# Grouped-query attention between two adapter layers: keys turned by blocks on VectorE, softmax sums divided out of the output, rotary table loaded per unit, four weight stage slots

## The reference

```
x += down(silu(gate(x)) * up(x))            # layer 0, F = 1376, each with a rank-16 adapter chosen per sequence
q, k, v = x Wq', x Wk', x Wv'               # layer 1: 32 query heads, 8 key heads, D = 128
q, k = rope(rmsnorm(q)), rope(rmsnorm(k))   # positions: length of the sequence + token
keys = [paged cache: 16 pages of 32, through a table; k]      # 640 keys, those past the length masked
x += softmax(q keys' / sqrt(D)) [cached v; v] Wo'
x += x (W2 quantised by group, codebook, + adapter)'          # layer 2, 512 x 512
x += x W3[adapter]'                                           # layer 3, one of 8 matrices
```

## Time and profile before

| | |
|---|---|
| median of 3 runs | 1479.15 us (1478.11 to 1483.87) |
| the profiled execution | 1478.15 us, its span 1476.5 us |
| mean granted TensorE clock | 0.985 |
| layer 0 up to the first projection of q | 276.7 us |
| 64 units, to the last step's end | some 1137 us |
| layers 2 and 3 | some 62 us |

### The profile page before, as it was taken

The page is one execution under the profiler, slowest core; times in us unless marked ns, Lnnn a source line. Parts: engine busy times, 40 slices in busy tenths (PEclk is TensorE's granted clock), DMA queues, the critical chain, the costliest instruction groups (busy, mean ns, idle before and its releaser), DMA issues.

```text
span 1476.5 us, 26919 instructions
## 1 busy us (share of the span) xinstructions
PE 1407.4 (95%) x8068; PEld 1218.9 (83%) x8068; DVE 1147.7 (78%) x2779; ACT 994.3 (67%) x1985; POOL 504.4 (34%) x688
## 2 busy tenths in 40 slices
PE   6998998789999999999999999999999999999888
PEld 5776776568888888888888888888888888888767
DVE  4885666467788788888888888788888878888756
ACT  5664663366677777767777776777777777777643
POOL 5321221245434333334433333343333434333200
PEclk9999999889999999999999999999999999999999
DMA  8776765324321111212111211121111212110224
GB/s 191 245 236 188 247 186 161 101 83 136 116 72 43 58 47 42 62 41 59 57 54 34 65 44 51 36 65 45 58 51 37 61 47 58 51 37 29 101 77 152
DMA packets 102852, 130.01 MB, mean 88 GB/s; under 512 B 11973, under 2 KB 78150, under 8 KB 97334
## 3 DMA queue, kind: packets, MB, share of 16 engines
q1 hardware_dynamic: 97184, 108.70, 23.7%
q0 software_dynamic: 5376, 19.60, 4.7%
q10 hardware_dynamic: 150, 0.01, 0.0%
HBM read 125.11 MB, written 36.72 MB: 110 GB/s over the span
## 4 chain that ended last, share of the span: by engine, by line
PE 78%; DVE 8%; ACT 5%; issue 4%; DMA 3%; POOL 1%; POOLq 1%; SPq 0%; ACTq 0%; DVEq 0%
PE proj_ps L1278 18%; PE sc L1318 15%; PE o_ps L1355 14%; PE proj_ps L1376 12%; PE ring L1337 9%; PE o_ps L1089 2%; PE ring L1391 2%; PE ring L1403 2%; PE proj_ps L1089 2%; PE sc L1089 2%; ACT wb L725 2%; DMA prep<-scale_dram 1%; DMA wd_raw<-in_WdT 1%; DVE pTl L1837 1%; DVE wb L1546 1%
## 5 line engine op out<-in xcount | busy, mean ns | idle before, releaser
L1837 DVE TENSOR_TENSOR pTl<-ring,pTh 128x512 fp32r<-128x512 f32 x320 | 215.1, 689 | 79.1 <-ACT pTh L914 74.1
L896 ACT ACTIVATE p_sb<-p_sb,bias,rstd 128x640 f32<-128x640 f32 x256 | 235.8, 921 | 43.8 <-DVE bias L1813 43.8
L649 POOL TENSOR_TENSOR rstd<-var,half_neg 128x4 f32<-128x4 f32 x64 | 86.0, 1344 | 493.7 <-DVE var L1874 493.7
L914 ACT ACTIVATE pTh<-ring 128x512 fp32r<-128x512 f32 x320 | 184.4, 599 | 53.1 <-PE ring L1337 52.3
L1803 DVE CUSTOM_DVE_ANT_0 p_sb<-sc,mask 128x640 f32<-128x640 f32 x256 | 209.2, 817 | 2.5 <-PE sc L1318 2.1
L1337 PE MATMUL ring<-ident,p_sb 128*128 128x128 f32 x1280 | 182.1, 273 | 5.5 <-DVE p_sb L1829 3.0
L1278 PE MATMUL proj_ps<-wh,xh 128*128 128x512 f32 (+1 forms) x512 | 179.6, 351 | 0.7 <-ACT q_sb L941 0.7
L1337 PEld LDWEIGHTS ring<-ident,p_sb 128*128 128x128 f32 x1280 | 153.4, 141 | 32.6 <-DVE p_sb L1829 3.7
L1278 PE MATMUL proj_ps<-wl,xh 128*128 128x512 f32 (+1 forms) x512 | 173.1, 338 | 0.0
L1278 PE MATMUL proj_ps<-wh,xl 128*128 128x512 f32 (+1 forms) x512 | 172.6, 337 | 0.0
L1318 PE MATMUL sc<-kTh,qTh 128*128 128x320 f32 x512 | 164.4, 321 | 2.5 <-DVE kTl L1938 2.5
(11 more groups left out here) (242 smaller groups left out, 3696.4 us busy)
## 6 DMA issues: line engine op xcount, KB each, us to landing
k_pages<-in_k_cache SPq DMA_DIRECT2D x128, 128.0 KB, 3.1
v_pages<-in_v_cache POOLq DMA_DIRECT2D x128, 128.0 KB, 3.2
k_raw<-k_pages SPq DMA_DIRECT2D x64, 256.0 KB, 3.0
v_raw<-v_pages SPq DMA_DIRECT2D x64, 256.0 KB, 2.9
stage<-in_Wqkv SPq DMA_DIRECT2D x32, 384.0 KB, 3.5
w_raw<-in_WguT SPq DMA_DIRECT2D x19, 512.0 KB, 5.1
stage<-in_WoT SPq DMA_DIRECT2D x32, 256.0 KB, 3.4
w_raw<-in_W3T SPq DMA_DIRECT2D x8, 1024.0 KB, 5.0
```

Source lines behind the costliest of these rows:

```text
L896: act_e.activation(p_sb[:, p_slot(u, h), :], p_sb[:, p_slot(u, h), :], ACT.Exp, bias=bias[:, h:h + 1], scale=rstd[:, u.k % 2, h:h + 1], ac ...
L914: act_e.activation(pTh[:, c, :], ring[c % 2][:, :], ACT.Copy).then_inc(S["pth"], 1)
L1837: v.tensor_tensor(pTl[:, c, :], ring[c % 2][:, :], pTh[:, c, :].bitcast(F32), ALU.subtract).then_inc(S["ptl"], 1)
```

## The change

- Cached keys are no longer transposed by PE. `load_k` brings them in four DMAs that place each 32x32 block where it belongs after transposing, in runs of 32 floats; DVE's block transpose (`turn_cached_k`) turns the blocks inside; ACT makes the high half from SBUF, POOL the low half.
- P is not normalised. One reciprocal of all four sums per unit goes to DRAM (`put_inv`, 2 KB), comes back as one row on all partitions (`spread_inv`, 256 KB), is laid out by ACT (`lay_inv`), and DVE multiplies PV's result by it in PSUM (`norm_o`) before its halves are made.
- The biases of the exps are made in pairs (`shift`).
- The rotary table goes to DRAM (2 MB, in `load_group(0)`) and comes back by unit (`load_rope`, 256 KB), a step ahead.
- q times cos, k times cos and the sum of k move from DVE to POOL, the scale of k from DVE to ACT. POOL's page copies stand behind the power for k and the cached keys' low half, three, and one at the step's end.
- `stage` has four slots. Low halves of Wqkv chunks 0 and 1 and of Wo heads 2 and 3 of later heads are POOL's. Matmuls that need low halves stand last in their group.
- SP copies nine key pages per step; loads of keys are issued a step earlier.

```diff
-        stage = l1_sb("stage", [P, 2, QKV])
+        stage = l1_sb("stage", [P, C, QKV])
...
+                    sp.dma_start(rope_dram, rope_tab[:, :, :, :]).then_inc(S["rope_in"], 16)
...
-                sp.dma_start(k_raw[:, :, :], of_head(k_pages, u)).then_inc(k_load, 16)
+                pages = k_pages[u.seq, :, :, :].rearrange("(i r) h d -> r i (h d)", r=PSIZE)
+                for j in range(D // PSIZE):
+                    sp.dma_start(k_raw[j * PSIZE:(j + 1) * PSIZE, :].rearrange("r (i c) -> r i c", c=PSIZE),
+                                 pages[:, :, bass.ds(u.head * D + j * PSIZE, PSIZE)]).then_inc(k_load, 16)
...
             def step(u):                                   # SP
-                load_out(u + -3, 3)
-                load_out(u + -1, 0)
-                if u.exists() and (u.k > 0):
-                    load_k(u)
-                load_in(u + 4, 0)
-                load_out(u + -1, 1)
-                if (u + -1).exists() and (u.k > 1):
+                put_inv(u + -2)
+                if (u + -1).exists() and u.k > 1:
                     load_v(u + -1)
-                load_in(u + 1, 2)
-                load_in(u + 1, 3)
-                load_in(u + 4, 1)
-                load_out(u + -1, 2)
+                load_next_out(u)
+                spread_inv(u + -2)
+                if (u + 1).exists():
+                    load_rope(u + 1)
+                    load_k(u + 1)
+                load_next_in(u)
                 if u.k < B - 1:
-                    copy_keys(8)
+                    copy_keys(9)
...
+            def put_inv(u):
+                if u.exists():
+                    sp.wait_ge(S["inverted"], u.count(1, 1))
+                    sp.dma_start(inv_dram[u.k % 2], inv[:, u.k % 2, :]).then_inc(S["inv_put"], 16)
+
+            def spread_inv(u):
+                if u.exists():
+                    sp.wait_ge(S["inv_put"], u.count(16, 16))
+                    sp.dma_start(inv_row[:, :], inv_dram[u.k % 2].rearrange("t h -> (t h)").partition_broadcast(P)
+                                 ).then_inc(S["inv_in"], 16)
...
+            def lay_inv(u):                                # ACT
+                if not u.exists():
+                    return
+                act_e.wait_ge(S["inv_in"], u.count(16, 16))
+                if (u + 2).exists():
+                    act_e.wait_ge(S["qrope"], (u + 2).count(1, 1))
+                act_e.activation(inv_wide[:, :].rearrange("p (h t) -> p h t", h=REP),
+                                 inv_row[:, :].rearrange("p (t h) -> p h t", h=REP), ACT.Copy).then_inc(S["inv_laid"], 1)
...
+            def norm_o(u):                                 # DVE
+                if not u.exists():
+                    return
+                dve.wait_ge(S["pv"], u.count(KC, KC))
+                dve.wait_ge(S["inv_laid"], u.count(1, 1))
+                v.tensor_tensor(o_ps[:, :], o_ps[:, :], inv_wide[:, :], ALU.mult).then_inc(S["on"], 1)
...
+            def turn_cached_k(u):                          # DVE
+                if not u.exists():
+                    return
+                dve.wait_ge(k_load, u.count(4 * 16, 4 * 16))
+                if u.back(1):
+                    dve.wait_ge(S["kcl"], u.count(1, 0))
+                v.transpose(k_turned[:, :], k_raw[:, :]).then_inc(S["kcT"], 1)
...
             def step(u):                                   # DVE
                 mean_square_q(u + -1)
-                invert(u + -2, 2)
-                normalise(u + -2, 0)
-                invert(u + -2, 3)
-                new_wo(u + -2, 0)
-                normalise(u + -2, 3)
+                invert(u + -2)
                 mask_max(u + -1, 0)
...
                 low_pt(u + -2, 0)
                 low_pt(u + -2, 1)
-                cos_q(u)
...
-                cos_k(u)
+                turn_cached_k(u)
                 low_pt(u + -2, 2)
...
                 low_pt(u + -2, 4)
...
+                norm_o(u + -2)
+                mask_max(u + -1, 2)
                 low_o(u + -2)
-                mask_max(u + -1, 2)
                 low_q(u)
-                invert(u + -1, 1)
                 low_new_k(u)
                 mask_max(u + -1, 3)
+                shift(u + -1, 1)
                 add_y(u + -2)
```

More of the change, by code:

```diff
@@ L290, in cond_resid_kernel @@
         v_page_in = [sem(f"v_page_in_{b}") for b in range(B)]
-        stage_in = [sem(f"stage_in_{n}") for n in range(2)]
+        stage_in = [sem(f"stage_in_{n}") for n in range(C)]
         k_load = sem("k_load")
@@ L479, in _ @@
[L479 to L484, removed]
-                if u.new_head():
[L486 to L490, removed]
-            def load_in(u, c):
-                if u.new_head():
-                    if c < 2:
-                        sp.wait_ge(S["wo_l"], (u + -1).heads(REP, c + 3))
-                    else:
-                        sp.wait_ge(S["wqkv_l"], u.heads(C, c - 1))
-                    load_wqkv(u, c)
@@ new lines, in _, with load_next_in @@
+                    load_rope(first)
+                if n in (6, 8):
+                    for h in (n - 6, n - 5):
+                        sp.wait_ge(S["wqkv_l"], h + 1)
+                        load_wo(first, h)
+            def load_next_in(u):
+                if 0 <= u.k < UNITS - B and u.seq == HALF:
+                    sp.wait_ge(S["wo_l"], REP + 2 * u.head)
+                    if u.head:
+                        sp.wait_ge(S["w_low_pool"], 4 * u.head)
+                    for c in range(C):
+                        load_wqkv(u + HALF, c)
@@ new lines, in load_next_out @@
+            def load_next_out(u):
+                if u.new_head():
+                    sp.wait_ge(S["w_low_pool"], 4 * u.head - 2)
+                    sp.wait_ge(S["wqkv_l"], C + 2 * u.head)
+                    for h in range(REP):
+                        load_wo(u, h)
+            def put_inv(u):
[7 more added lines that the diff above has]
+                                 ).then_inc(S["inv_in"], 16)
@@ L644, in turn_and_norm @@
                                    ALU.pow).then_inc(S["k_pow"], 1)
+                pool.wait_ge(S["kch"], u.count(1, 1))
+                pool.tensor_tensor(kTl[:, u.k % 2, 0:L], k_turned[:, :], kTh[:, u.k % 2, 0:L].bitcast(F32), ALU.subtract
+                                   ).then_inc(S["kcl"], 1)
+                if u.k < B - 1:
+                    copy_values(3)
+                for c in range(2):
+                    low_w(u + 1, c)
+                for h in range(2, REP):
+                    low_wo(u + -2, h)
                 pool.wait_ge(S["q_var"], u.count(1, 1))
@@ L972, in square_k, with scale_k @@
                 if u.back(1):
-                    act_e.wait_ge(S["k_ss"], u.count(1, 0))
+                    act_e.wait_ge(S["q_ss"], u.count(1, 0))
                 act_e.activation(sq_k[:, :], k_sb[:, :], ACT.Square).then_inc(S["k_sq"], 1)
+            def scale_k(u):
+                if not u.exists():
+                    return
+                act_e.wait_ge(S["ksum"], u.count(1, 1))
+                act_e.wait_ge(S["k_pow"], u.count(1, 1))
+                act_e.activation(k_cos[:, :], k_cos[:, :], ACT.Copy, scale=rstd[:, u.k % 2, REP:REP + 1]
+                                 ).then_inc(S["krope"], 1)
             def slot_free(u):
@@ L1353, in attend @@
                     high, low = vnh[:, u.k % 4, :], vnl[:, u.k % 4, :]
-                for k, (a, w) in enumerate(((high, pTh), (high, pTl), (low, pTh))):
+                for k, (a, w) in enumerate(((high, pTh), (low, pTh), (high, pTl))):
+                    if k == 2:
+                        pe.wait_ge(S["ptl"], u.count(KC, c + 1))
                     i = mm(o_ps[:, :], a, w[:, c, :], start=c == 0 and k == 0, stop=c == KC - 1 and k == 2)
```

347 lines of the change are left out of this document (164 added, 183 removed).

## The result

The changed kernel takes 1470.21 us (median of 5 runs, 1467.72 to 1470.68); the kernel before took 1481.09 in the same comparison. The ratio is 0.9921, 95% interval 0.9901 to 0.9941: 0.8% faster, where 2.5% was forecast. The profiled execution is 1467.99 us (span 1466.0), so 10.2 us were gained of 37.5.

A forecast was written before the change was run, and what follows sets the result against it. PE was taken as the bound, busy 95% of the span, a steady step being 17.20 us of its instructions. Gains 27.3 + 4.3 + 2.4 + 5 - 3 + 1.5 = 37.5 us gave 1441 us; range 1428 to 1465.

The forecast's parts named there:

- Part 1: Steady attention steps: four key transposes leave PE, 0.44 us a unit over 62 units, 27.3 us gained.
- Block transpose: On DVE where cos_q and cos_k stood: taken as 0.7 us, up to 1.4 us costing nothing.
- the round trip in a plain step: Sums through DRAM: broadcast lands 6.5 to 9.0 us into the step, lay_inv done by 9.7, cover 0.5 before output.
- Rivals 2 to 5: Small wait each step, chance 0.10; DRAM round trip bounds, 0.05; long block transpose, 0.04; key load outlasts cover, 0.03.
- rival 3: Steady steps: the sums' round trip through DRAM becomes the bound, each step 1.7 us longer, 1546 us; chance 0.05.
- First two steps: First two attention steps: page copies leave POOL's path ahead of the power for k, 4.3 us gained in two.
- end of layer 0: With four stage slots SP passes and PE's waits for wd_h shrink: 5 us gained, bounds 0 and 5.9.
- table store: Rotary table's 2 MB to DRAM shortly before the hole at 110 us: 3 us lost, between 0 and 5.7.
- The drain: Last unit: normalisations leave the path, norm_o and round trip are added; 1.5 us gained, between 3 gained and 2 lost.
- The next six: Six steps after the first two: page copies no longer hold scale_k and low_o, 2.4 us gained of 2.9 excess.
- Rival 1: Only the transposes count; table store, traffic and new queues eat what the edges give: 1451 us, chance 0.17.
- The waits of a new head I leave as they are: Steps that start a new head: their waits were taken as unchanged, no term in the sum.

The follow-up runs named there:

- e7: Changed kernel with PE making the four transposes of P's last chunk twice: plain steps 17.19 us, median 1490.6 us.
- e9: Kernel before with only DVE's block transpose of cached keys and POOL's low half of them added: 1487.1 us, ratio 1.0040 to before.
- e2: Changed kernel with the first steps' nine page copies made one or two DMAs from fixed addresses: steps 2 to 7 100.5 us, median 1453.9 us.
- e10: Changed kernel, head steps with broadcast first, POOL waiting for DVE, PE's low-half products last; 18 page copies at layer 0's end, six a step: 1442.16 us.
- e1: Changed kernel with SP issuing the broadcast of the sums ahead of the four Wo loads in head steps: head step 18.24 us, median 1462.1 us.
- e12: Changed kernel, head steps only: SP's broadcast ahead of v and Wo loads, POOL's low half of v waits for DVE's Wqkv low halves: 1458.8 us.
- e3: Changed kernel with POOL's low half of v waiting for DVE's two low halves of Wqkv in head steps: 1483.4 us.

## Why the prediction was wrong in size

The direction and most steps held; two failed, and they cost 28.0 us, of which the other places gave 1 back: 27 are missing.

- *Part 1, 0.44 us a unit*: right, in 48 of 55 steps and by e7. But part 1 took it as PE's alone; e9 shows that it needs other parts of the change, of which DVE's relief is the one that its trace points to.
- *Block transpose, key and rotary loads, POOL's queue, the round trip in a plain step*: right: 0.70, 2.5, 3.3 us, no wait of PE. POOL was free 11.0 into the step, for 11.3 in the prediction, whose own terms give 10.8. Rivals 2 to 5 did not come in plain steps. But what rival 3 describes, a round trip that ends too late and norm_o behind it, is what happened in the head steps and in five of steps 2 to 7. The 2 KB write took 1.4, half of my 2.9; lay_inv 1.12 and not 0.6, hidden in a plain step.
- *First two steps, end of layer 0, table store*: 4.4 for 4.3. The waits for wd_h, 5.9 us before, are gone. At the hole near 110 us PE waits 7.7 us for `prep` in place of 6.3, so the table store cost about 1.4 there for the 3 taken. The start moved by 2.4 for 2; since kernels whose layer 0 is the same start from 274.3 to 276.6, these small terms are confirmed in sign and no more. The drain less: it took 106.0 here, 108.5 before, and 105.6 to 109.1 in the runs made from the changed kernel with nothing added, so its 1.5 is not shown.
- *"The next six", failed*: 2.4 gained over the transposes, with "nothing" as the bound below, was the term; with the transposes' 2.6 that is +5.0, and -8.3 was measured. I priced there the copies that leave POOL's path. Rival 1 even had the mechanism, nine copies of 1.2 us with the write behind them, and called it 1 us late. I did not add SP's queue as I had DVE's and POOL's: nine copies 11, four key loads 3, the rest about 2 is 16 us of a 16.75 us step, with a wait of 2.3 for the write's landing in between, and in step 4 three loads of Wqkv, 1.7, on top. The write was 4.3 late in step 4. e2 and e10 give the term back.
- *"The waits of a new head I leave as they are", failed*: a term put at nothing cost 14.3 us net, about 2.0 a head. One part is an order: SP's spread_inv behind a wait for low halves and 1 MB (1.0 a head, e1). The other is two engines at once (1.08, e12): before, DVE had no low half of Wqkv beside POOL's low half of v; now both subtract at the head of the step. The trace agrees here with the Trainium skill (page "SBUF — State Buffer", section "Who interferes with whom"), which says that a DVE instruction with two inputs in SBUF contends with a POOL instruction reading SBUF; it was there to be weighed for a change that puts DVE's subtractions beside POOL's. The kernel before had shown it too, on the engine that could afford it: seven times a low half of Wqkv on DVE fell beside POOL's k times sin, which had started just after it. DVE's took 0.96 us as always, POOL's 1.09 in place of 0.32.

The range, 1428 to 1465, had room for a small wait in every step, not for two places of 13.3 and 14.7 us.

## What to carry to other kernels

Add up a queue's issue time like an engine's busy time: a new wait put at its head inherits all that stands before it, and the steps to look at are those that are not like the others (first units, new heads). Work that leaves the bounding engine shortens a step only if the engine that takes it has room at that place in its order (e9). And mend an order before a contention: e3 lost 13 us where e12, with the broadcast first, gained 11.

## What the hardware showed beside this

A page copy whose address comes from a register holds SP 1.2 us; one DMA from a fixed address for up to nine pages held it 0.5 to 0.8 us, with all traffic of those steps at 154 GB/s. ACT's copy of 128x512 is 0.60 us from PSUM and 0.62 from contiguous SBUF, but 1.12 when it reads SBUF in steps of 16 bytes; DVE's multiply goes from 0.70 to 1.09 with that operand. Where DVE's and POOL's subtractions met, one of 128x768 on DVE took 2.04 us for 0.95, and the one of 128x512 on POOL 2.03 for 1.29. And idling costs PE twice: in steps 2 to 7 its 602 instructions took 106.67 us where they take 100.51 without a wait, 4.1 of this in steps 4 and 5 alone, at a granted clock of 0.92, so partly at 1.2 GHz after PE had idled. The clock is not all of it: steps 3 and 6 take 17.2 us each for 16.75 at a clock of 1.00.
